# A chain of attention and feed-forward layers on one core: the linear attention's value and output weights multiplied into one, its copies in a new order, and the shift of the residual sent tile by tile

## The reference, cut to what matters

```python
q = x @ Wq.T; k = x @ Wk.T; v = x @ Wv.T        # 8 heads of 128 columns each
q = rms_norm(q) * qk_gain;  k = rms_norm(k)
attn = softmax(mask(q @ k^T / sqrt(128)))       # inside chunks of 64 rows
y = attn @ v + q @ state                        # state: earlier chunks, decayed
y = y.reshape(rows, 8 * 128) @ Wo.T
```

```python
x = x + o @ wo
h = shift_token(x)        # columns 64 to 127 come from the row before
h = (h - mean(h)) / sqrt(var(h) + 1e-5) * g + b
x = x + (a * gelu(g2)) @ w2 + b2,   where a, g2 = split(h @ w1 + b1)
```

## Time and profile before

| what | value |
|---|---|
| median of 3 runs | 2173.48 us (2167.74 to 2177.42) |
| profiled execution, its own time | 2174.38 us |
| its span (first to last instruction) | 2172.2 us |
| PE, DVE, ACT, POOL busy | 74%, 60%, 50%, 40% of the span |
| mean granted PE clock | 0.861 of full speed |
| DMA queues | 36.49 MB, hardware queue 5.6% of 16 engines |

### The profile page before, as it was taken

One profiled execution on the slowest core, in us unless ns is written; L12 is line 12 of the kernel. 1 busy time (PEld: TensorE's weight loads), 2 busy tenths in 40 slices (PEclk: granted clock), 3 DMA queues, 4 the chain that ended last, 5 costly groups with the idle time before them and its releaser, 6 DMA issues. The chain is left out here.

```text
span 2172.2 us, 37710 instructions
## 1 busy us (share of the span) xinstructions
PE 1611.1 (74%) x13333; PEld 1148.2 (53%) x13333; DVE 1305.1 (60%) x3712; ACT 1084.7 (50%) x2729; POOL 875.8 (40%) x628
## 2 busy tenths in 40 slices
PE   6999997789899747898777898988411104948685
PEld 5888885566666523344444666666300004736464
DVE  2454444887777434556747877775387774636544
ACT  3656663687777514664435778876110101324332
POOL 1332323776656212234536766664045360221102
PEclk9999998999999967998868999999755555969878
DMA  4000000111111000000000111110000000000001
GB/s 184 1 1 1 1 1 8 23 33 26 24 28 24 20 1 1 1 1 1 1 1 20 29 28 28 29 26 21 5 0 0 0 0 0 16 24 1 1 6 54
DMA packets 31078, 36.49 MB, mean 17 GB/s; under 512 B 19120, under 2 KB 21168, under 8 KB 30512
## 3 DMA queue, kind: packets, MB, share of 16 engines
q1 hardware_dynamic: 29872, 32.01, 5.6%
q0 software_dynamic: 1024, 2.10, 0.3%
HBM read 12.08 MB, written 3.15 MB: 7 GB/s over the span
## 5 line engine op out<-in xcount | busy, mean ns | idle before, releaser
L945 ACT ACTIVATE arena<-ps 128x512 f32<-128x512 f32 (+4 forms) x686 | 374.4, 605 | 296.8 <-PE ps L318 126.3
L318 PE MATMUL ps<-consts,arena 128*128 128x128 f32 x400 | 84.4, 358 | 265.9 <-DVEq L1747 139.8
L318 PEld LDWEIGHTS ps<-consts,arena 128*128 128x128 f32 x400 | 58.9, 181 | 296.9 <-DVEq L1747 141.6
L1180 ACT ACTIVATE arena<-ps 128x320 f32<-128x320 f32 (+4 forms) x256 | 132.5, 561 | 137.4 <-PE ps L676 134.5
L1080 ACT ACTIVATE arena<-arena,g_small 128x128 f32<-128x128 f32 x512 | 199.1, 404 | 0.5
L1512 DVE CUSTOM_DVE_ANT_0 arena<-ps,consts,g_ss 128x128 f32<-128x128 f32 x512 | 145.5, 347 | 78.4 <-PE ps L482 75.1
L2031 POOL TENSOR_TENSOR arena<-arena,consts 128x512 f32<-128x512 f32 (+1 forms) x64 | 93.5, 1461 | 195.8 <-ACT arena L1180 195.8
L2052 POOL TENSOR_TENSOR arena<-arena 128x512 f32<-128x512 f32 x64 | 82.0, 1282 | 181.1 <-DVE arena L1520 181.1
L2105 POOL TENSOR_TENSOR arena<-arena 128x2048 f32<-128x2048 f32 x16 | 109.5, 6842 | 99.7 <-DVE arena L1739 99.7
L676 PE MATMUL ps<-arena 32*128 32x160 f32 (+4 forms) x1024 | 122.3, 468 | 21.1 <-ACT arena L1180 10.5
L1519 DVE TENSOR_TENSOR arena<-ps,tabs 128x512 f32<-128x512 f32 x128 | 87.7, 685 | 50.3 <-ACT arena L1049 42.8
(11 more groups left out here) (252 smaller groups left out, 4192.9 us busy)
## 6 DMA issues: line engine op xcount, KB each, us to landing
arena<-arena SPq DMA_DIRECT2D x112, 128.0 KB, 2.3
weights<-in_w SPq DMA_DIRECT2D x1, 5069.0 KB, 24.5
weights<-in_w SPq DMA_DIRECT2D x1, 2052.0 KB, 12.9
arena<-Y SPq DMA_DIRECT2D x16, 128.0 KB
arena<-Y SPq DMA_DIRECT2D x16, 127.0 KB
consts<-in_c SPq DMA_DIRECT2D x1, 1278.0 KB, 9.0
out<-X SPq DMA_DIRECT2D x1, 1024.0 KB, 5.1
sorted_rows<-arena,e_idx POOLq DMA_INDIRECT x32
```

What stands on the lines that cost most here:

```text
L318: last = tr(ps[:, bank, j * P:(j + 1) * P], src(j), ident)
L945: copy = lambda o, i: act.activation(o, i, ACT.Copy)
L1180: act.activation(b_p[:, U % 2, 2 * gp:2 * gp + 2, at:at + n], ps[:, b:b + 2, 0:n], ACT.Exp, scale=float(HD) ** -0.5).then_inc(s.b_exp, 1)
```

## The change

It has three parts.

1. In the linear attention the product of each head's value weights and output weights is computed once at the start (`fold_weights`: two halves of four heads, each 4 transposes, a copy, 4 matmuls, a copy). The values then come out already multiplied by the output weights. `mix` uses the decayed probabilities as the stationary operand, in 10 matmuls of 128 columns, and adds up over the heads of a batch in bank 6. `keep_y` and `out_rows` are gone.
2. `project_v` moves from bank 2 to bank 7, where `turn_x`, `gates` and `decays` now work too; these now wait for `keep_values` of the step (semaphore a_vin).
3. On ACT the order becomes `keep_q`, `keep_probs`, `keep_k`, `squares`, and on PE `turn_probs` stands ahead of `turn_k`. In the windowed block the shift is issued for each tile, the 127-partition copy first, behind that step's `lookback`; the waits count 176 in place of 48 for a group.

```diff
+                def fold_weights(half):
+                    for k in range(4):
+                        h = 4 * half + k
+                        last = tr(ps[:, 3, k * P:(k + 1) * P], W("a_qkv", 2048 + h * P, 2048 + (h + 1) * P), ident)
+                    last.then_inc(s.a_wT_ps, 1)
+                    pe.wait_ge(s.a_wT, half + 1)
+                    need(pe, s.a_vo, half)
+                    for k in range(4):
+                        h = 4 * half + k
+                        last = mm(ps[:, 4, k * P:(k + 1) * P], a_wT[:, k, :], W("a_wo", h * P, (h + 1) * P),
+                                  start=True, stop=True)
+                    last.then_inc(s.a_vo_ps, 1)
...
                 def decays(t):
                     z = (t + 2) // HA
                     pe.wait_ge(s.a_decay, z + 1)
-                    need(pe, s.a_yT, heads_by(t - 1))
+                    pe.wait_ge(s.a_vin, t + 3)
...
                 def project_v(n):
                     z, h = n // HA, n % HA
-                    need(pe, s.a_kT, n)
+                    need(pe, s.a_vin, n)
+                    pe.wait_ge(s.a_xT, begun(n - 3, -4))
+                    pe.wait_ge(s.a_gate_in, begun(n - 3, -3))
+                    need(pe, s.a_gamma, begun(n - 3, -2))
+                    pe.wait_ge(s.a_vo, h // 4 + 1)
                     for j in range(NT):
-                        last = mm(ps[:, 2, j * P:(j + 1) * P], a_xT[:, z % 2, j * P:(j + 1) * P],
-                                  W("a_qkv", 2048 + h * P, 2048 + (h + 1) * P), start=True, stop=True)
+                        last = mm(ps[:, 7, j * P:(j + 1) * P], a_xT[:, z % 2, j * P:(j + 1) * P],
+                                  a_vo[:, h, :], start=True, stop=True)
...
                 def mix(n):
...
-                    for i in range(NT):
-                        last = mm(ps[:, 6, i * P:], a_v[:, n % 4, i, :], a_mt[:, n % 2, i, 0:(NT - i) * P],
-                                  start=i == 0, stop=i == NT - 1, skip_group_check=True)
-                    last.then_inc(s.a_y, 1)
-
-                def out_rows(n):
...
+                    for i in range(NT):
+                        for j in range(i, NT):
+                            last = mm(ps[:, 6, j * P:(j + 1) * P], a_mt[:, n % 2, i, (j - i) * P:(j - i + 1) * P],
+                                      a_v[:, n % 4, i, :], start=h == i == j == 0, stop=h == HA - 1,
+                                      skip_group_check=True)
+                    last.then_inc(s.a_y, 1)
...
+                    if head(t):
+                        turn_probs(t)
                     if head(t + 1):
                         turn_k(t + 1)
-                    if head(t):
-                        turn_probs(t)
-                    if head(t - 1):
-                        out_rows(t - 1)
+                    if -3 <= t < -1:
+                        fold_weights(t + 3)
                     if head(t + 2):
                         project_v(t + 2)
...
-                    if head(t - 1):
-                        keep_y(t - 1)
                     if head(t + 1):
                         keep_q(t + 1)
+                    if head(t):
+                        keep_probs(t)
+                    if head(t + 1):
+                        keep_k(t + 1)
                     if head(t + 2):
                         squares(t + 2)
-                    if head(t + 1):
-                        keep_k(t + 1)
-                    if head(t):
-                        keep_probs(t)
+                    if -3 <= t < -1:
+                        fold_weights(t + 3)
...
-                    dve.wait_ge(s.a_wo, HA * (z + 1))
-                    tt(stream(z), stream(z), ps[:, 7, :].rearrange("p (j d) -> p j d", j=NT), ALU.add)\
+                    dve.wait_ge(s.a_y, HA * (z + 1))
+                    tt(stream(z), stream(z), ps[:, 6, :].rearrange("p (j d) -> p j d", j=NT), ALU.add)\
...
-                def shift(g):
-                    z = NT * (g % NB)
-                    sp.wait_ge(gs.add, n0 + NT * g + NT)
-                    need(sp, gs.h2, m0 + g)
-                    sp.dma_start(g_h[:, :, 0:64], Y[:, z:z + NT, 0:64]).then_inc(gs.sh, 16)
-                    sp.dma_start(g_h[1:P, :, 64:128], Y[0:P - 1, z:z + NT, 64:128]).then_inc(gs.sh, 16)
-                    sp.dma_start(g_h[0:1, 1:NT, 64:128], Y[P - 1:P, z:z + NT - 1, 64:128]).then_inc(gs.sh, 16)
+                def shift(n):
+                    N, i, j = n0 + n, n % TT, n % NT
+                    sp.wait_ge(gs.add, N + 1)
+                    need(sp, gs.h2, m0 + n // NT)
+                    sp.dma_start(g_h[1:P, j, 64:128], Y[0:P - 1, i, 64:128]).then_inc(gs.sh, 16)
+                    sp.dma_start(g_h[:, j, 0:64], Y[:, i, 0:64]).then_inc(gs.sh, 16)
+                    if j < NT - 1:
+                        sp.dma_start(g_h[0:1, j + 1, 64:128], Y[P - 1:P, i, 64:128]).then_inc(gs.sh, 16)
 
                 sp.wait_ge(gs.zero, F + 1)
                 for t in range(-4, TILES + 9):
-                    if at_step(t, 5):
-                        shift((t - 5) // 4)
                     if live(t + 2):
                         lookback(t + 2)
+                    if live(t - 2):
+                        shift(t - 2)
```

More of the change, by code:

```diff
@@ L325, in turn_x @@
                     pe.wait_ge(gs.ln, z + 1)
-                    need(pe, s.a_yT, heads_by(t - 1))
+                    need(pe, s.a_vin, t + 3)
                     for j in range(NT):
-                        last = tr(ps[:, 6, j * P:(j + 1) * P], Y[:, NT * z + j, :], ident)
+                        last = tr(ps[:, 7, j * P:(j + 1) * P], Y[:, NT * z + j, :], ident)
                     last.then_inc(s.a_xT_ps, 1)
@@ L333, in gates @@
                     pe.wait_ge(s.a_xT, z + 1)
-                    need(pe, s.a_yT, heads_by(t - 1))
+                    need(pe, s.a_vin, t + 3)
                     for j in range(NT):
-                        last = mm(ps[:, 6, j * HA:(j + 1) * HA], a_xT[:, z % 2, j * P:(j + 1) * P], W("a_wg"),
+                        last = mm(ps[:, 7, j * HA:(j + 1) * HA], a_xT[:, z % 2, j * P:(j + 1) * P], W("a_wg"),
                                   start=True, stop=True)
@@ L377, in turn_q @@
                     pe.wait_ge(s.a_qn, n + 1)
-                    pe.wait_ge(s.a_vin, n + 1)
+                    need(pe, s.a_kT, n)
                     for j in range(NT):
@@ L413, in mix @@
                 def mix(n):
+                    z, h = n // HA, n % HA
                     pe.wait_ge(s.a_pT, n + 1)
@@ L416, in mix @@
                     pe.wait_ge(s.a_vin, n + 1)
-                    need(pe, s.a_yT, n)
-                    pe.wait_ge(s.a_xT, begun(n, -4))
-                    pe.wait_ge(s.a_gate_in, begun(n, -3))
-                    pe.wait_ge(s.a_gamma, begun(n, -2))
-                    for i in range(NT):
-                        last = mm(ps[:, 6, i * P:], a_v[:, n % 4, i, :], a_mt[:, n % 2, i, 0:(NT - i) * P],
-                                  start=i == 0, stop=i == NT - 1, skip_group_check=True)
-                    last.then_inc(s.a_y, 1)
-                def out_rows(n):
-                    z, h = n // HA, n % HA
-                    pe.wait_ge(s.a_yT, n + 1)
                     if h == 0:
                         need(pe, s.a_add, z)
-                    for j in range(NT):
-                        last = mm(ps[:, 7, j * P:(j + 1) * P], a_yT[:, n % 2, j * P:(j + 1) * P],
-                                  W("a_wo", 128 * h, 128 * h + 128), start=h == 0 and j == 0, stop=h == HA - 1,
-                                  skip_group_check=True)
-                    last.then_inc(s.a_wo, 1)
+                    for i in range(NT):
[4 more added lines that the diff above has]
+                    last.then_inc(s.a_y, 1)
                 for t in range(-4, HEADS + 1):
@@ L952, in keep_x @@
                     need(act, s.a_v, HA * (z - 1))
-                    copy(a_xT[:, z % 2, :], ps[:, 6, :]).then_inc(s.a_xT, 1)
+                    copy(a_xT[:, z % 2, :], ps[:, 7, :]).then_inc(s.a_xT, 1)
                 def log_gates(t):
@@ L983, in keep_raw, with fold_weights @@
                         .then_inc(s.a_raw, 1)
-                def keep_y(n):
-                    act.wait_ge(s.a_y, n + 1)
-                    need(act, s.a_wo, n - 1)
-                    copy(a_yT[:, n % 2, :], ps[:, 6, :]).then_inc(s.a_yT, 1)
+                def fold_weights(half):
+                    act.wait_ge(s.a_wT_ps, half + 1)
+                    need(act, s.a_vo_ps, half)
+                    copy(a_wT, ps[:, 3, :].rearrange("p (h d) -> p h d", h=4)).then_inc(s.a_wT, 1)
+                    act.wait_ge(s.a_vo_ps, half + 1)
+                    copy(a_vo[:, 4 * half:4 * half + 4, :], ps[:, 4, :].rearrange("p (h d) -> p h d", h=4))\
+                        .then_inc(s.a_vo, 1)
                 def keep_q(n):
@@ L1014, in keep_values @@
                     need(act, s.a_y, n - 3)
```

(4 more changed lines are left out.)

15 lines of the change are left out of this document (7 added, 8 removed).

## The result

| what | before | changed |
|---|---|---|
| median of 5 runs each, same chip | 2173.48 us (2165.38 to 2177.71) | 2193.88 us (2190.89 to 2197.71) |
| ratio, 95% interval | | 1.009 (1.0075 to 1.0106) |
| profiled execution, its own time | 2174.38 us | 2190.89 us |
| its span | 2172.2 us | 2188.8 us |

The change costs 20.4 us, more than the half per cent that can be told apart, where 2181 had been forecast. By medians the forecast is 13 us low, and the value lies inside the range, near its upper end.

The account below looks back on a forecast made before the run. Before the change, PE's work was taken to bound each linear attention step, and a DMA wait the windowed block's tails. 2174.4 + 19.8 (linear attention) - 12.8 (shift) = 2181.4, forecast 2181 us, range 2168 to 2196.

Parts of the forecast that it names:

- first step: Linear attention, between the first scores: the 8.05 us step, pipe not yet full, becomes a full one, +1.7 us.
- the ring: Linear attention: the loop squares, sums, roots, normalise, division, transposes, copies back to squares sets a plain step, 9.34 to 9.73 us.
- PE stays the bound: Faster rival, linear attention: PE's work still sets the step, -0.81 us in each of 31 steps; 2143 us, chance 0.08.
- Right: the shift: Windowed block: tile-by-tile issue removes DVE's 6.4 us DMA wait at each of two tails, -12.8 us.
- The rival that gave the 6.58 us to the one-partition DMA: Slower rival, windowed block tails: that small DMA holds SP, so only 3 us gained per tail; 2188 us, chance 0.10.
- Batch boundaries: Linear attention, three boundaries of three steps: bank 7 work waits for keep_values, 35.5 against 33.2 us, +2.3 each, +6.9.
- two short dips: Linear attention: dips of PE's clock that came before and may come or not, some 4 us of spread.
- The rival of the clock: Slower rival, linear attention: PE's holes lower its clock below 0.88, steps reach 10.4 us at 0.82; 2200 us, chance 0.13.
- start and end: Linear attention: first fold and delayed values +3.0 us (between 0 and 6.8); a copy and a product gone at the end, -1.5.
- No change: Whole kernel: time within half a per cent, 10.9 us of 2173.5, about what can be told; chance 0.50.
- slower: Whole kernel: time above 2184.4 us, the bound of half a per cent; chance 0.42.
- its own case: Whole kernel: the main forecast, 2181 us with a spread of 2172 to 2191, given 0.69.

## Why the prediction came out as it did

The linear attention, term by term, from the distances between scores. A stretch of 6.8 us at half clock does 3.4 us of work, so it loses 3.4.

| term | predicted | measured |
|---|---|---|
| first scores (the fold) | +3.0 | +5.0 (36.62 to 41.63) |
| first step | +1.7 | +2.5 (8.05 to 10.60) |
| 17 plain steps and the statistics and sums of a batch | +6.6 and +1.5 | +7.5 (158.7 to 166.2) |
| three boundaries, four steps each | +8.1 | +16.6 (132.8 to 149.4) |
| last step before the end | +0.4 | +2.0 (7.68 to 9.68) |
| end | -1.5 | -0.4 |
| sum | +19.8 | +33.2 |

**Right: the ring.** A plain step was to go from 9.34 to 9.73 and is 9.68 to 9.73. PE waits for POOL before `turn_probs`, by 0.40 us where 0.5 to 1 had been named as the sign. Each link agrees within 0.02 us, the order alone makes it, and taking the order back unmakes it. That "PE stays the bound" did not happen is settled by the same rows.

**Right: the shift.** Two waits of 6.4 us went and the windowed blocks are 6.3 and 8.0 us shorter. The rival that gave the 6.58 us to the one-partition DMA fell with its row of 0.59 us. The prediction named the rule of the Trainium skill (DMA: Bandwidth & Descriptors, "Why a DMA increments its semaphore by 16 and not by 1"), that a copy over 127 partitions runs on one engine; by that rule the long DMA is the 127-partition one. The rows agree: the DMA share of 0.07 is about one engine of 16, and the 15 GB/s moved meanwhile are far more than the 768 bytes of the one-partition DMA, so the long copy was still running. That SP was held because of it is read from these rows; a run with only that DMA cut was not made.

**Wrong: "Batch boundaries", +2.3 each: the clock was put at nothing.** In the three boundaries 27.2 us lie at half clock, for 10.2 before, which is 13.6 lost for 5.1: **+8.5 us, two thirds of the 13.4 by which the stage missed**. The prediction gave "two short dips" some 4 us of spread, as chance, though its own working had PE wait for a copy ahead of the decays with nothing left to do. The filled hole shows that behind a hole of 2.99 us it is cause and not chance: with it closed, all three stretches behind the decays are gone.

The waits came out right as a sum, and partly by luck. Take the half-clock stretches away and the four steps were 42.5, 42.6 and 42.6 us before and are 45.2, 45.5 and 45.1 now, +2.7 each; by hand, with the plain step behind them, they were to be 45.3. But two of the four were wrong and cancel. The step that ends in `turn_x` was to be 10.35 us and is 11.6 to 11.9: by hand PE reaches `turn_probs` 6.66 us after the scores, with no wait, and in fact the ring still holds it there and makes it 7.8:

```profile
81.67 1.13 PE L413 MATMUL ps<-arena 128*128 128x128 f32 x8
...
89.48 0.66 PE L428 MATMUL ps<-consts,arena 128*128 128x128 f32 x4 [0.39 <-POOL arena L1979]
```

The step behind the decays was counted as a plain one of 9.73, held by the ring; it is 8.5 without half clock (8.55 with the hole filled), PE's own pace; the long step before it would let the ring get ahead, which is read from the order and not tried apart. The other two, 10.8 for `gates` and 14.2 to 14.3 for the decays, are as worked out.

**The rival of the clock was half right.** It put the loss in the plain steps, from a clock below 0.88 on, and gave 2200. In the plain steps the clock stays 1.00, though PE waits in each. The Trainium skill (TensorE: Matmul & The Clock Gate, "A second HAM failure mode: psum-queue depth-cycling") speaks of a clock that goes up and down when PE idles briefly but often. The plain steps do not show that, with some 1 us of holes in each at full clock; beyond the first step of the pipe, half-clock stretches begin only at the boundaries, by the holes of 1.34 us ahead of `gates` and 2.99 us ahead of the decays, and not behind each of the former. That the time came out nearer to this rival's than to the forecast is due to that other place.

**Mis-sized: start and end.** The fold was worth 3.0 within 0 and 6.8; leaving it out moves the first scores by 6.0, and the mean of the four profiles with it lies 5.6 later than that of the four without, so little of it was covered: the second fold delays the values and, by a hole of 2.03 us, the decays. In the stretches that the clock column shows, the start and the first step have 10.2 us at half clock for 6.8, 1.7 us of loss more. At the end I took off a copy and a product (-1.5) from a step that had been 7.68, PE having no projections left there; but the ring runs through ACT's copy of k for the last head too, and the step is a full 9.68. The two terms together were to be -1.1 and are +1.6, 2.7 us.

**The chances.** "No change" had 0.50 and "slower" 0.42, and slower it was, 0.94%, with an interval that leaves out both no difference and the half per cent. The median lies 2 us below the upper end of the range and above the 2172 to 2191 that the prediction gave as the spread of its own case. So the ring and the sign of the sum were right, but that the time fell inside the range is owed to the room left for rivals that did not happen as described.

## What to carry to other kernels

Before a producer is moved behind a consumer on an in-order engine, write down the ring through all engines that this closes and add up its links from the trace: that sum was good to 0.05 us here, and it, not the busiest engine, was the step. When a wait opens a hole on PE ahead of small products, price the clock behind it as well as the hole: the same boundary cost 2.7 us by its waits and up to 5.1 by half clock. A sum that comes out right should be checked step by step all the same: here 1.3 us too little in one step hid 1.2 us too much in another. And an engine that has been relieved of work shows the next wait only then: the change beyond the shift gained 6.5 us until three products were moved into a wait of 0.42 us, and 26.8 with them (medians; some 4 us of that last gain are half-clock time and an unchanged block).

## What the runs showed of the hardware that was not expected

- More work on PE made the kernel faster: 14 products without use in a hole of 2.99 us took 9.4 us off the time, with the granted clock behind it at 1.00 for 0.50.
- A hole is not the whole story: 0.99 us ahead of the decays had no half clock behind it at that boundary of the kernel before, but the same 0.99 us had 6.8 and 3.4 us behind it at the other two boundaries of the same execution. Six products in a hole of about 2 us left all three stretches; with the mix split as well, where the hole is 1.31 us, they closed it, and one stretch of 3.4 us stayed behind it. From which hole on the clock falls is not settled by these runs.
- The profile's clock column does not show half pace at the very start: it reads 1.00 for 18 to 22 us of the kernel before, yet the 16 records of L364 that begin at 19.11 take 3.76 us, and 2.02 us from 40.06 on.
- Such stretches can take part of a gain back: without the fold the first scores came 6.0 us earlier and the stage ended 4.6 us earlier, with 3.4 us more at half clock in the boundaries.
- The issue of a DMA of 768 bytes held SP for 6.58 us behind a 127-partition copy of 508 pieces, and one of 256 bytes for 0.59 us behind a copy of 127 pieces, cut to a quarter.
